# Moving the first attention unit of each chunk into the chunk before, in a two-layer local-attention program on one core

## The reference

```python
def _layer(x, wqkv, qs, ksc, wo, lg, lb, w1, b1, w2, b2):   # x: 4 sequences x 1024 x 256
    h = shift_token(x)
    q, k, v = jnp.split(h @ wqkv, 3, axis=-1)               # 8 heads of 64
    q, k = rotary_xpos(l2norm(q) * qs, l2norm(k) * ksc)
    sim = einsum(q * 8, [keys of the block before, own block])   # window 128, masked
    o = softmax(sim) @ [values of the block before, own block]
    x = x + o @ wo
    h = layer_norm(shift_token(x)) * lg + lb
    a, g = jnp.split(h @ w1 + b1, 2, axis=-1)               # hidden 682
    return x + (a * gelu(g)) @ w2 + b2
```

## Time and profile before

| | |
|---|---|
| median of 3 runs | 1930.73 us (1926.85 to 1933.4) |
| the profiled execution's own time | 1927.33 us |
| its span, first to last instruction | 1925.2 us |
| mean granted TensorE clock | 0.984 |
| the layers' chunks, first and last "out" on DVE | 776.8 to 1922.0 us |

### The profile page before, as it was taken

The page is one execution under the profiler, slowest core; times in us unless marked ns, Lnnn a source line. Parts: engine busy times, 40 slices in busy tenths (PEclk is TensorE's granted clock), DMA queues, the critical chain, the costliest instruction groups (busy, mean ns, idle before and its releaser), DMA issues.

```text
span 1925.2 us, 47714 instructions
## 1 busy us (share of the span) xinstructions
PE 1823.5 (95%) x17808; PEld 1565.2 (81%) x17808; DVE 1231.2 (64%) x4126; ACT 1374.2 (71%) x3998; POOL 881.4 (46%) x1302
## 2 busy tenths in 40 slices
PE   6999999999999879999999999999999999999998
PEld 4788788788778658888898897888888888889787
DVE  5543544445443357777777777787777777777765
ACT  5886978788688556857758668677576685775864
POOL 3533543344243455536436355364473553654631
PEclk9999999999999979999999999999999999999999
DMA  4321321322223620111101101314112112010110
GB/s 148 101 77 44 113 87 54 91 96 88 74 91 99 210 69 23 48 42 32 51 26 45 57 15 53 107 33 163 45 40 64 34 48 65 23 59 26 43 48 29
DMA packets 125018, 128.11 MB, mean 67 GB/s; under 512 B 26632, under 2 KB 100082, under 8 KB 124788
## 3 DMA queue, kind: packets, MB, share of 16 engines
q1 hardware_dynamic: 121620, 118.77, 19.9%
q10 hardware_dynamic: 3168, 6.29, 1.0%
HBM read 72.44 MB, written 36.85 MB: 57 GB/s over the span
## 4 chain that ended last, share of the span: by engine, by line
PE 75%; ACT 10%; DVE 6%; POOL 3%; DMA 2%; SPq 2%; issue 1%; DVEq 0%; POOLq 0%; ACTq 0%
PE f_bank L1454 18%; PE a_bank L630 16%; PE f_bank L1593 10%; PE f_scores L1608 5%; PE f_o_bank L1568 5%; PE a_o_bank L727 4%; PE f_scores L1535 4%; ACT f_prob L1677 3%; PE f_bank L1546 3%; PE a_bank L712 2%; PE a_scores L704 2%; PE f_bank L1507 2%; POOL a_prob L610 2%; PE f_bank L1550 1%; DVE f_u L1817 1%
## 5 line engine op out<-in xcount | busy, mean ns | idle before, releaser
L1418 POOL TENSOR_SCALAR f_prob<-f_prob,f_row_inv 128x192 f32<-128x192 f32 x512 | 224.4, 457 | 391.9 <-DVE f_row_inv L1759 391.9
L610 POOL TENSOR_SCALAR a_prob<-a_prob,a_row_inv,a_gate 128x128 f32<-128x128 f32 x512 | 226.3, 459 | 377.5 <-DVE a_row_inv L948 377.5
L1454 PE MATMUL f_bank<-weights,f_actT 128*128 128x512 f32 x1152 | 300.8, 407 | 1.6 <-DVE f_actT L1710 1.6
L1593 PE MATMUL f_bank<-f_hT,f_w 128*128 128x256 f32 x2112 | 269.1, 283 | 1.1 <-DVE f_gu L1813 1.1
L1593 PEld LDWEIGHTS f_bank<-f_hT,f_w 128*128 128x128 f32 x2112 | 258.5, 188 | 4.1 <-DVE f_gu L1813 2.7
L1454 PEld LDWEIGHTS f_bank<-weights,f_actT 128*128 128x128 f32 x1152 | 210.8, 191 | 46.9 <-DVE f_actT L1710 1.8
L1677 ACT ACTIVATE f_prob<-f_scores,f_neg_max 128x192 f32<-128x192 f32 x512 | 208.0, 427 | 17.7 <-DVE f_neg_max L1751 16.4
L1406 POOL TENSOR_TENSOR f_qk_tok<-f_qk_tok,tables 128x512 f32<-128x512 f32 x128 | 164.5, 1305 | 116.3 <-DVE f_sin_part L1727 116.3
L1697 ACT ACTIVATE f_u<-f_gu 128x256 fp32r<-128x256 f32 x192 | 80.2, 418 | 174.1 <-DVE f_gu L1813 174.1
L1400 POOL TENSOR_TENSOR f_norm<-f_norm,f_minus_half 128x16 f32<-128x16 f32 x64 | 187.7, 2933 | 32.2 <-DVE f_norm L1719 31.4
L838 ACT ACTIVATE a_prob<-a_scores,a_neg_max 128x128 f32<-128x128 f32 x512 | 179.4, 391 | 24.1 <-DVE a_neg_max L939 24.0
(11 more groups left out here) (143 smaller groups left out, 3958.6 us busy)
## 6 DMA issues: line engine op xcount, KB each, us to landing
split_weights<-a_hi_lo SPq DMA_DIRECT2D x16, 512.0 KB, 3.0
x_next<-states SPq DMA_DIRECT2D x32, 256.0 KB, 3.2
tables<-scaled_tables SPq DMA_DIRECT2D x16, 512.0 KB, 5.9
f_x<-states SPq DMA_DIRECT2D x16, 512.0 KB, 5.1
split_weights<-a_hi_lo SPq DMA_DIRECT2D x12, 682.0 KB, 4.7
weights<-split_weights ACTq DMA_DIRECT2D x6, 1024.0 KB, 9.5
f_w<-split_weights SPq DMA_DIRECT2D x4, 1280.0 KB, 10.7
f_v_crossed<-f_v SPq DMA_DIRECT2D x40, 128.0 KB, 2.4
```

Of the source, the lines that this page charges most:

```text
L610: last = nc.gpsimd.tensor_scalar(part, part, row_inv[:, a % 2, head, t:t + 1], gate[:, half, t, h:h + 1], ALU.mult, ALU.mult)
L1418: last = nc.gpsimd.tensor_scalar(part, part, row_inv[:, a % 2, head, t:t + 1], 1.0, ALU.mult, ALU.mult)
L1454: last = nc.tensor.matmul(out, lhs(c, a), rhs(c, b), start=(i == 0), stop=(i == len(order) - 1))
L1593: mm = nc.tensor.matmul(out[:, which * PART:(which + 1) * PART], w1[:, wp, c, col:col + P], hT[:, hp, c, columns_of(a // FH)], start=(i == ...
```

## The change

Unit 0 of a chunk gets its scores, softmax and weighting in the preceding chunk, as unit 8 (16 for the second half, `a == NU`) of that chunk's lists; `program_of` renames it to unit 0 of the next chunk, and the opening does it for the very first one. ("scores", 8) stands between ("down", 9) and ("down", 10) on PE. On ACT ("softmax", 8) stands before ("transpose_qk", 3), on DVE ("scores", 8) and ("weigh", 8) behind ("out", 1). ("transpose_qk", 3) goes behind ("down", 11) on PE, "load_x" goes between ("out", 0) and ("out", 1) on SP. The scores wait for the copies of the tiles that they read (tiles 0 and 1 for units 0 to 3, all from unit 4 on) instead of for all copies.

```diff
-SYNC_ORDER = [("load_x", 0), ("load_x1", 0), ("load_tables", 0), ("load_others", 0), ("shift_front", 0), ("shift_keys", 0),
-              ("shift_back", 0), ("cross_values", 0), ("add_attended", 0), ("out", 0), ("out", 1)]
+SYNC_ORDER = [("load_x1", 0), ("load_tables", 0), ("load_others", 0), ("shift_keys", 0), ("shift_front", 0), ("shift_back", 0),
+              ("cross_values", 0), ("add_attended", 0), ("out", 0), ("load_x", 0), ("out", 1)]
-SCALAR_ORDER = [("softmax", 0), ("softmax", 1), ("transpose_x", 0), ("transpose", 0), ("softmax", 2), ("transpose", 1), ("project_qk", 0),
+SCALAR_ORDER = [("softmax", 1), ("transpose_x", 0), ("transpose", 0), ("softmax", 2), ("transpose", 1), ("project_qk", 0), ("softmax", 3),
...
-                ("transpose_h", 1), ("up", 4), ("up", 5), ("up", 6), ("up", 7), ("up", 8), ("up", 9), ("transpose_qk", 2), ("up", 10),
-                ("up", 11), ("transpose_qk", 3), ("load_wqkv", 0)]
+                ("up", 4), ("up", 5), ("up", 6), ("up", 7), ("up", 8), ("up", 9), ("transpose_qk", 2), ("load_wqkv", 0), ("up", 10),
+                ("up", 11), ("softmax", 8), ("transpose_qk", 3)]
-VECTOR_ORDER = [("scores", 0), ("scores", 1), ("weigh", 0), ("weigh", 1), ("transpose_x", 0), ("scores", 2), ("scores", 3), ("weigh", 2),
+VECTOR_ORDER = [("scores", 1), ("weigh", 1), ("transpose_x", 0), ("scores", 2), ("scores", 3), ("weigh", 2), ("project_qk", 0),
...
-                ("up", 8), ("up", 9), ("rope_sum", 3), ("up", 10), ("up", 11), ("out", 0), ("out", 1)]
+                ("up", 9), ("rope_sum", 3), ("up", 10), ("up", 11), ("out", 0), ("out", 1), ("scores", 8), ("weigh", 8)]
...
-                ("down", 5), ("down", 6), ("transpose_qk", 2), ("up", 10), ("up", 11), ("down", 7), ("down", 8), ("transpose_qk", 3),
-                ("down", 9), ("down", 10), ("down", 11)]
+                ("transpose_h", 1), ("up", 4), ("down", 3), ("up", 5), ("up", 6), ("up", 7), ("down", 4), ("up", 8), ("down", 5), ("up", 9),
+                ("transpose_qk", 2), ("down", 6), ("up", 10), ("up", 11), ("down", 7), ("down", 8), ("down", 9), ("scores", 8),
+                ("down", 10), ("down", 11), ("transpose_qk", 3)]
...
+            opening = before + [(kind, NU) for kind, i in order if kind in F_ATTENTION and i == UNITS]
+            program = flat([(None, opening), *((it, steps) for it in range(SEQUENCES - 1)), (SEQUENCES - 1, last)])
+
+            return [(0 if it is None else it + 1, kind, 0) if kind in F_ATTENTION and a == NU else (it, kind, a) for it, kind, a in program]
...
-                    if s == 0:
-
-                        pe.wait_ge(copied.sem, copied.past(it, ("transpose_qk", half * TILES - 1), 1) if half else copied.upto(it, -1))
-                        if half:
-                            pe.wait_ge(keys_shifted.sem, keys_shifted.past(it, ("shift_keys", 0)))
+                    if s % PAIRS == 0:
+
+                        pe.wait_ge(copied.sem, copied.past(it if half else before_it, ("transpose_qk", (half or HALVES) * TILES - (1 if s else 3)), 1))
+                    if s == 0 and half:
+                        pe.wait_ge(keys_shifted.sem, keys_shifted.past(it, ("shift_keys", 0)))
                     elif s == 1:
                         pe.wait_ge(x2_ready.sem, x2_ready.upto(it, 2 * half - 1))
```

More of the change, by code:

```diff
@@ L991 @@
 F_PREPARE = ("load_wqkv", "load_tables", "transpose_x", "project_qk", "rope", "rope_sum", "transpose_qk", "project_v", "cross_values")
+F_ATTENTION = ("scores", "softmax", "weigh")
 F_FIRST_HALF = ("shift_keys", "load_wqkv", "load_others")
[L993 to L1006, removed]
@@ new lines @@
+ORDER = [("softmax", 1), ("scores", 1), ("scores", 2), ("weigh", 1), ("transpose_x", 0), ("transpose", 0), ("softmax", 2), ("transpose", 1),
+         ("scores", 3), ("weigh", 2), ("project_qk", 0), ("load_x", 0), ("take_o", 0), ("softmax", 3), ("values", 0), ("values", 1),
+         ("load_x1", 0), ("weigh", 3), ("rope", 0), ("scores", 4), ("transpose", 2), ("project_qk", 1), ("softmax", 4), ("scores", 5),
+         ("weigh", 4), ("rope_sum", 0), ("values", 2), ("transpose", 3), ("project_qk", 2), ("softmax", 5), ("scores", 6), ("values", 3),
+         ("weigh", 5), ("rope", 1), ("transpose_qk", 0), ("take_o", 1), ("transpose", 4), ("scores", 7), ("softmax", 6), ("weigh", 6),
+         ("project_qk", 3), ("project_o", 0), ("rope_sum", 1), ("weigh", 7), ("transpose", 5), ("softmax", 7), ("load_tables", 0),
+         ("load_others", 0), ("shift_keys", 0), ("shift_front", 0), ("shift_back", 0), ("take_o", 2), ("values", 4), ("values", 5),
+         ("transpose", 6), ("project_v", 0), ("transpose_qk", 1), ("transpose", 7), ("ln_stats", 0), ("ln_apply", 0), ("take_o", 3),
+         ("rope", 2), ("values", 6), ("values", 7), ("project_v", 2), ("transpose_h", 0), ("project_o", 1), ("rope_sum", 2), ("up", 0),
+         ("up", 1), ("up", 2), ("project_v", 1), ("ln_stats", 1), ("ln_apply", 1), ("down", 0), ("down", 1), ("project_v", 3), ("up", 3),
+         ("down", 2), ("transpose_h", 1), ("cross_values", 0), ("rope", 3), ("load_wqkv", 0), ("up", 4), ("down", 3), ("up", 5), ("up", 6),
+         ("up", 7), ("down", 4), ("up", 8), ("up", 9), ("rope_sum", 3), ("down", 5), ("down", 6), ("transpose_qk", 2), ("up", 10),
+         ("up", 11), ("down", 7), ("down", 8), ("add_attended", 0), ("transpose_qk", 3), ("down", 9), ("out", 0), ("out", 1), ("scores", 8),
+         ("down", 10), ("down", 11), ("softmax", 8), ("weigh", 8)]
@@ L1100, in is_prepared @@
         def is_prepared(kind, a):
-            return kind == "load_x" or kind in F_PREPARE and (a >= (HALVES - 1) * PER_CHUNK[kind] or kind == "load_wqkv")
+            return kind == "load_x" or kind in F_ATTENTION and a == NU or kind in F_PREPARE and (a >= (HALVES - 1) * PER_CHUNK[kind] or kind == "load_wqkv")
         e, t0 = HALVES - 1, (HALVES - 1) * TILES
```

44 lines of the change are left out of this document (23 added, 21 removed).

## The result

The changed kernel takes 1948.59 us (median of 4 runs, 1942.57 to 1950.36) against 1929.76 us of the kernel before in the same session (4 runs): ratio 1.0091, 95% interval 1.0062 to 1.012. The forecast was 1932.0 with a range of 1917 to 1942. It is slower by three times the 0.3% bound, and outside the range.

A forecast was written before the change was run, and what follows sets the result against it. PE, busy 95%, was taken as the bound, except at chunk boundaries, bound by ACT's queue. 1927.3 (profiled execution) + 10.2 (fifteen boundaries at 0.68) - 5.8 (clock) = 1931.7, plus 0.3 for the median: 1932 us, range 1917 to 1942.

The forecast's parts named there:

- The chain through ACT: At each chunk boundary, ACT's copies between the exponentials of units 0 and 1 delay unit 3's scores by 0.60 us.
- unit 2's scores at t = 3.14: PE at a boundary, t = 0 where DVE begins ("out", 1): start at 3.14 instead of 3.59, 0.45 us won.
- The 0.08 us of PE's work: PE before t = 0: 0.87 us of scores replace 0.79 us of transposes, +0.08 us a boundary.
- The small reorders: Moved down projections, ("up", 9) and load_wqkv: 0, at most 0.2 us either way, load_wqkv once at most 1.5 us.
- I take the clock as kept ... 5.8 us: Behind boundaries PE's clock no longer falls, giving back 0.83 us at seven of them, 5.8 us in all.
- The row that it rested on: Attention phase: PE waits for a_v four times, 2.0 us at the longest, with clock 1.00 from 50 to 650 us.
- Rival 1: Behind boundaries the clock falls as before: 1937.5 us, with the median's offset up to 1941, slower; chance 0.20.
- Cost 0, with 1.4 us of cover: SP's moved load of x lands at t = 3.8; its transposes could start as late as 5.2, so no cost.
- Rival 3: At boundaries x lands after t = 5.2 and PE, ACT and DVE wait: 1940 to 1955 us, slower; chance 0.08.
- the two rivals: Rival 1, clock falling behind boundaries (chance 0.20), and Rival 3, x landing late at boundaries (chance 0.08).

The follow-up runs named there:

- x early with fill: Changed kernel with the load of x back at the start of SP's list, plus 10 and 10 useless PE transposes in its boundary stalls: 1929.40 us, ratio 1.0002.
- before with fill: Kernel before plus 12 useless identity transposes on PE in the stall ahead of unit 2's scores: 1922.07 us, ratio 0.9956.
- Experiment 1: Changed kernel with only the load of x moved back to the start of SP's list: 1944.86 us against 1926.72, ratio 1.0096.
- the fills: Four kernels given useless PE transposes in the boundary stalls, among them the kernel before: 1922.07 us with them, 1930.08 without.
- x early: Same run as Experiment 1: changed kernel with the load of x back at the start of SP's list, 1944.86 us, ratio 1.0096.
- experiment 2: Kernel before with only the load of x moved between ("out", 0) and ("out", 1) on SP: 1945.9 us, ratio 1.0103.
- x first: Kernel before with 10 useless PE transposes per boundary and the transposes of x moved to the start of the chunk: 1924.61 us, ratio 0.9985.
- the fastest kernel: As x first, but unit 0's scores between ("down", 9) and ("down", 10), its exponentials behind the copies, and 8 useless transposes: 1915.23 us, ratio 0.9936.

## Why the prediction was wrong

- **The chain through ACT: right.** Forecast: unit 2's scores at t = 3.14, unit 1's exponentials at 4.0, unit 3's scores at 8.49. Measured: 3.15, 4.06, 8.47. Without low clock it costs 0.57 us a boundary (x early with fill against before with fill), forecast 0.60. The 0.08 us of PE's work lies ahead of t = 0, where it is part of the 1.5 us of the chunks. From the first ("out", 1) to the end that makes 9.7 us, small reorders included, against 10.2.
- **The small reorders: nearly right.** Forecast at nothing, at most 0.2 us each; the chunks of after take 1.7 us more, 1.1 of which could be the 0.08 us a chunk above. Not tested one by one.
- **"I take the clock as kept ... 5.8 us": wrong, the first step that failed.** Low stretches stayed, 8 of 14 instead of 7. The row that it rested on was also misread. Of the four waits for a_v in the earlier trace rows, only three (1.3, 1.5 and 1.3 us) lie in the stretch from 50 to 650 us with clock 1.00. The one of 2.0 us ends at 41.79, and behind it the clock falls (low from 43.2 on; the row is for 42 to 50 us):

```profile
41.79 1.17 PE L712 MATMUL a_bank<-ident,a_prob 128*128 128x128 f32 x8 [1.98 <-ACT a_v L791]
```

```profile
42.00:50.00 8.00, 8.00 (x61) 6.34 (x59) 4.79 (x31) 7.73 (x26) 3.61 (x9) 0.79 0.02 4
```

This part of the program is the same in all thirteen kernels here. Behind the three shorter stalls the clock falls in none of their traces, behind this one in three, and behind another of 2.0 us (PE waits for DVE's a_o until about 644) in seven. So single stalls of up to 1.5 us did keep the clock, but the new order has two, 1.5 and 1.4 us with 2.5 us of work between. Experiment 1 shows what such a pair does with x in time (8 of 14), and the fills show the stalls to be the cause. The Trainium skill (TensorE: Matmul & The Clock Gate, "What's actually happening"), weighed in the prediction, has throttled as the default and a monitor that runs free of the program; by that rule nothing was to be given back, and the traces agree (7 before, 8 after, 0 with fill).
- **The size of a fall: also wrong.** Rival 1 had 0.83 us, with a word that a later fall costs more. Before's own seven cost 0.93 on average, and in the new order with x early it is 1.54.
- **"Cost 0, with 1.4 us of cover" for the load of x: wrong, the second step.** Two parts of it failed. The issues came later than at t = 0 and 0.4: at 0.64 and 1.07 at the boundary shown, at 0.30 to 0.43 and 0.73 to 0.87 at the other 13. The store of ("out", 0) is issued at t = -0.19 to -0.08 instead of -0.5. And the landing was taken at its median of 3.4, from loads issued behind ("transpose_x", 0), where it was 4.0 with 5.6 at the longest between two stores of "out", 10.6 in experiment 2 beside weight loads. That makes 4.8 with the median landing and up to 6.4, so the cover to 5.2 is gone at some boundaries and not at others. Rival 3 named the mechanism, the reader and the point (t = 5.2), and had 0.08 as its chance.
- **The sum.** The chain 8.3 us, nothing back from the clock but 4.6 us more for later and dearer falls and the late load, and 2.4 us outside the boundaries: 1927.3 + 8.3 + 4.6 + 2.4 = 1942.6, against 1942.57 of the profiled execution (it is an account taken from that same trace, so it must come out). The forecast had +10.2 for the chain and -5.8 for the clock. The other three runs of after lie 5 to 8 us above it, with mean clocks of 0.981 and 0.982; more falls would explain it, but no trace of them was read. That the two rivals could come together, and that curing one would leave the whole loss, wasn't in the prediction.

**Still open:** why the landing of the same 256 KB varies from 2.9 to 5.6 us in after, and why, of boundaries alike to 0.03 us, some keep the clock and some lose it. Neither was tested. The traces' own record of the clock has a hint on the second: in before the low stretches behind the boundaries at 854.76, 1008.25, 1161.66 and 1315.22 start at 858.99, 1012.59, 1166.19 and 1319.79, 153.60 us apart to 0.01, while the boundaries are 153.41 to 153.56 apart. That looks like a grid in time of the clock's own, and whether a stall meets it well or badly would depend on where the chunk happens to lie. If so, a count such as 7, 8 or 11 of 14 is partly luck of the chunk's length, and only 0 against 7 or 8 is a strong result.

## What to carry to other kernels

Before an instruction or a DMA is moved next to the path that sets the end, put its latest landing, not the median, against the reader, and look at what else is on the queues there. When two things fill the same stall (here late data and a clock that falls for lack of work), one of them taken away alone can show nothing, as in the order of after: test both together. And where TensorE must stand still for a microsecond or two again and again, useless matmuls into a free bank can keep the clock; here 12 of them cost no time that could be seen (11.69 us for an undisturbed boundary with and without) and were worth 0.44%.

## What the runs showed of the hardware

- A stall of 1.96 us a boundary lowers the granted clock (to the 1.2 GHz level) behind half of the boundaries; filled up so that 0.5 to 0.9 us of it are left, it does so behind none (before with fill, x first, and the fastest kernel). Single stalls of 1.3 to 1.5 us in the attention phase lowered it in none of thirteen traces, one of 2.0 us (at 40 us) in three of them, another of 2.0 us (at 642 us) in seven.
- A fall costs 0.2 or 0.3 us (after, x in time) and 0.72 to 1.38 us (before) where it lies among waits, and 1.54 us where it lies over dense matmuls (x early). The place of a fall matters as much as the number.
- A load of 256 KB behind a store on SP landed after 2.9 to 5.6 us (after), and after 10.6 us beside three weight loads of 1024 KB from another engine's queue: in that stretch the three kinds of transfer took 8.7 to 10.6 us in the median.
